# Routed tokens transposed one step ahead, and one spread of B and C for both halves of a state

## The chip, the cores and the metric

The kernel runs on one core of a Trainium2 chip. The metric is the device time of one launch in microseconds (us), the median of several runs. PE is TensorE (PEld its weight loads), DVE is VectorE, ACT is ScalarE, POOL is GpSimd, SP is SyncE. A line number L264 is a line of the kernel's file, as the profile gives it.

## What is computed

Two blocks on a residual stream x of 4 x 512 tokens, width 512. Each block adds a state-space layer over a context and then a feed-forward layer over the normalized x. The part in question is the second of these pieces together with the third: the mixture of experts of block 0, and the scan of block 1.

```
x = x + ssm0(ctx, layernorm(x))
x = x + moe(layernorm(x))       # shared expert + top 4 of 16 experts
x = x + ssm1(ctx, layernorm(x))
x = x + bitlinear_ffn(layernorm(x))

# ssm: per batch b, 512 channels, 16 states n, 512 time steps
u      = silu(conv(in_proj @ ctx))
delta  = softplus(dt_proj @ dt_lo + bias);  B, C = rows of x_proj @ u
state[e,n] = state[e,n] * exp(delta[e] * A[e,n]) + delta[e] * u[e] * B[n]
y[e]   = sum_n state[e,n] * C[n]  + D[e] * u[e]

# moe: token t, expert e of its top 4
out += coef[t,e] * (silu(x @ w1_e.T) * (x @ w3_e.T)) @ w2_e.T
```

B[n] and C[n] depend on the time step and not on the channel, so on the chip a row of 512 values is spread over 128 partitions before it is multiplied with a tile of channels.

## The kernel before

The kernel is a sequence of stages on one core, each with its own instruction order written out by hand for every engine; semaphores tie the engines together, and each engine takes its own queue strictly in order. The stages are the first scan (`ssm_first`, which also splits the expert weights into fp16 pairs and gets its C rows by DMA), a gate, the routing, `experts_and_ssm`, the combination of the routed outputs, a gate and the last feed-forward layer. The change lies in `experts_and_ssm` and in those parts of the class `Ssm` that the second scan uses; the branches with `alone` true belong to the first scan and keep their behaviour.

`experts_and_ssm` runs two things side by side. The feed-forward work is cut in slots: 88 slots of the shared expert (`NU`: 8 tiles of 256 tokens by 11 column pieces) and then 80 slots of routed steps g = 0 to 79 (`NSTEP`), each 128 gathered tokens of one expert. The scan work is cut in 148 entries, 37 for each of four batches, laid over the slots by `entry(slot)`: entries `at` 0 to 4 prepare a batch (in-projection, convolution, x_proj, dt, softplus), and 32 entries are the steps, one for each pair of a state n and a half of the channels (2 x 128 of 512). 68 entries lie in the shared slots, 58 of them steps; in the routed phase every slot has one, 70 of them steps, and two preparations begin at g = 6 and g = 43.

What a routed slot g does, by engine:

- PE: four fp32 transposes of the gathered tokens xg into the PSUM tile px (`x_transpose`, L1219); B of this scan step spread into pB by a matmul with a selector (`pe_spread_b`, L258); the down projection of step g-2 (L1227); three transposes of the hidden tile of g-1 (L1235, "hidden transposes" below); in a preparation the in-projection (`pe_in`); the up projection of g in 24 matmuls (L1246), in the middle of which C is spread into the same PSUM tile pB (`pe_spread_c`, L264); in a preparation then `pe_x` (L236) or `pe_dt` (L250).
- ACT: the high fp16 part of the tokens out of px (`x_hi`, L1333); the exponentials of the scan step (`act_exp`, L348); the copy of the down projection's result (L1349); the high part of the hidden tile (`h_hi`); the copy of C to SBUF (`act_c`, L341); tanh of the up result (L1343); then the preparation's work, such as `act_u` (L309), `act_z`, `act_e`, `act_ln`.
- DVE: the low part of the tokens (`x_lo`, L1446, reads px and xth); bu = du * B (`dve_bu`, L425); the scan (L434); the low part of the hidden tile (`h_lo`, L1451 and L1452); the two instructions of `silu_up` (L1457, L1460); then conv, split, delta and du (L413).
- POOL: the indirect fetch of the tokens of g+2 (L1149), the product of the scan's result with C (L471), the sum into U (L461).
- SP: the weights of the next expert into a ring of three, when an older expert is done.

The tiles xth and xtl exist once, px exists once, and the order of `x_transpose`, `x_hi`, `x_lo` and `up` is closed in one slot: `up(g)` waits for `x_lo(g)`. The shared slots have a similar chain with two buffers; four-transposes pieces there (`sx_transpose`, `sx_high`, `sx_low`) stand at the end of slots with column piece 4 or 7.

The scan step s is at first (batch, half, state): a batch goes through its 16 states for the first half of the channels and then for the second, so that B and C of a state are spread twice. B waits until the C before it is out of pB (`c_evac`), C waits until bu has read B (`bu_done`).

```
        def step(b, at):
            return b * STEPS + at - PRO, (at - PRO) // NS, (at - PRO) % NS
...
        pe.wait_ge(self.bu_done, s + 1)
        if not self.alone:
            pe.wait_ge(self.c_evac, s + 1)
```

## Time and profile before

| | |
|---|---|
| runs | 2286.73, 2280.6, 2284.96 us, median 2284.96 |
| profiled execution, its own time | 2281.42 us |
| its span in the trace | 2279.2 us |
| mean granted clock of PE | 0.876 |
| busy over the span | PE 1683.4 (74%), DVE 1759.7 (77%), ACT 1184.7 (52%), POOL 1336.8 (59%) |
| shared phase | about 797 to 1268 us |
| routed phase | about 1268 to 1896 us |

Busy shares over the span are means over stages with different limits; what a change in one stage is worth is read from that stage. In a timeline row a group of equal instructions in sequence is merged (x4), the us behind the start are the group's, and matmul times contain the drain, so the distance between starts is what a matmul holds PE for. PEclk in the table of stretches is the clock granted to PE as a share of 2.4 GHz.

### The profile page before, as it was taken

To read this page: it belongs to the slowest core of one execution; us is meant where nothing else is said; L and a number is where in the kernel's file an instruction comes from. 1 tells how busy PE (TensorE), PEld (TensorE's weight loads), DVE (VectorE), ACT (ScalarE), POOL (GpSimd) and SP (SyncE) were. 2 spreads that over 40 slices of the span, in tenths; PEclk is the share of its full clock that TensorE was granted. 3 is DMA by queue.
4 is the path that set the end of the run, shared out by engine and by line. 5 is a ranking of instruction groups with operands and counts; after the bars stand their busy time and mean duration, and the time that the engine had idled before them with its cause. 6 is when DMAs were issued, how large, how long until landed. Compare 5 with 4: busy or idle time off the path is not lost. (4 is left out here: it accounts for less than half of the span.)

```text
span 2279.2 us, 27596 instructions
## 1 busy us (share of the span) xinstructions
PE 1683.4 (74%) x8608; PEld 967.8 (42%) x8630; DVE 1759.7 (77%) x2275; ACT 1184.7 (52%) x1829; POOL 1336.8 (59%) x648
## 2 busy tenths in 40 slices
PE   4766756656536488999799988999889992005998
PEld 1222222212225445766467545666456661003554
DVE  4999999999955738887689847888478885757886
ACT  4675766757632034443444435555355551634776
POOL 0778778789950005775288815888258884653111
PEclk7878879889976588999899998999989996558999
DMA  6347456456544600001000333344424226650000
GB/s 213 132 149 236 149 169 222 152 177 223 182 143 134 144 24 10 11 13 35 5 10 30 135 113 137 121 157 159 144 95 157 81 75 249 210 170 1 24 24 28
DMA packets 127146, 264.65 MB, mean 116 GB/s; under 512 B 44546, under 2 KB 48386, under 8 KB 121794
## 3 DMA queue, kind: packets, MB, share of 16 engines
q1 hardware_dynamic: 93890, 184.24, 24.0%
q0 software_dynamic: 11520, 37.76, 5.8%
q10 hardware_dynamic: 21600, 40.90, 4.8%
q8 instruction: 78, 1.28, 0.2%
q14 instruction: 58, 0.48, 0.1%
HBM read 180.41 MB, written 82.44 MB: 115 GB/s over the span
## 5 line engine op out<-in xcount | busy, mean ns | idle before, releaser
L471 POOL TENSOR_TENSOR ssm_hs<-ssm_hs,ssm_Cs 128x1024 f32<-128x1024 f32 x128 | 314.9, 2461 | 144.7 <-DVE ssm_hs L434 140.7
L471 POOL TENSOR_TENSOR moe_hs<-moe_hs,moe_Cs 128x1024 f32<-128x1024 f32 x128 | 302.2, 2361 | 127.2 <-DVE moe_hs L434 96.1
L434 DVE TENSOR_TENSOR_SCAN moe_hs<-moe_dA,moe_bu 128x1024 f32<-128x1024 f32 x128 | 292.6, 2286 | 17.9 <-ACT moe_dA L348 8.4
L434 DVE TENSOR_TENSOR_SCAN ssm_hs<-ssm_dA,ssm_bu 128x1024 f32<-128x1024 f32 x128 | 292.8, 2287 | 17.4 <-ACT ssm_dA L348 0.5
L461 POOL TENSOR_TENSOR moe_U<-moe_U,moe_hs 128x1024 f32<-128x1024 f32 x128 | 302.0, 2360 | 5.9
L280 PE MATMUL ssm_pY<-ssm_hs,ssm_ident 128*128 128x512 f32 x512 | 276.9, 668 | 2.8 <-POOL ssm_hs L471 2.8
L1246 PE MATMUL moe_pgu<-all_Wreg,moe_xth 128*128 x1280 | 249.6, 318 | 31.4 <-DVE moe_xtl L1446 31.3
L1196 PE MATMUL moe_pgu<-moe_xsh,all_Wreg 128*128 128x256 f16 x1408 | 251.8, 277 | 10.9 <-DVE moe_hsl L1434 9.4
L258 PE MATMUL ssm_pB<-ssm_bc,ssm_sel 96*128 96x512 bf16 x128 | 54.9, 429 | 204.4 <-DVE ssm_bu L425 204.3
L1196 PE MATMUL moe_pgu<-moe_xsl,all_Wreg 128*128 128x256 f16 x704 | 195.0, 277 | 0.0
L666 POOL TENSOR_TENSOR ssm_wlo<-ssm_wst,ssm_whi 128x1360 f16<-128x1360 f32 x64 | 186.5, 2915 | 0.0
L348 ACT ACTIVATE ssm_dA<-ssm_dlt,ssm_A 128x511 f32<-128x511 f32 x256 | 169.0, 709 | 24.2 <-DVE ssm_hs L434 24.1
L348 ACT ACTIVATE moe_dA<-moe_dlt,moe_A 128x511 f32<-128x511 f32 x256 | 169.9, 714 | 18.3 <-DVE moe_du L413 18.3
L1246 PEld LDWEIGHTS moe_pgu<-all_Wreg,moe_xth 128*128 128x128 f16 x1280 | 127.0, 99 | 103.2 <-issue 36.9
L602 ACT ACTIVATE ssm_whi<-ssm_wst 128x1360 f16<-128x1360 f32 x64 | 85.5, 1336 | 155.4 <-DMA ssm_wst<-in_w_all 155.4
L425 DVE TENSOR_TENSOR ssm_bu<-ssm_du,ssm_pB 128x1024 f32<-128x1024 f32 x128 | 157.1, 1227 | 10.9 <-PE ssm_pB L258 0.8
L453 POOL TENSOR_TENSOR moe_U<-moe_U,moe_Dv 128x2048 f32<-128x2048 f32 x4 | 14.4, 3602 | 256.6 <-DVE moe_du L413 256.6
L425 DVE TENSOR_TENSOR moe_bu<-moe_du,moe_pB 128x1024 f32<-128x1024 f32 x128 | 156.3, 1221 | 6.8 <-PE moe_pB L258 6.7
L1196 PEld LDWEIGHTS moe_pgu<-moe_xsh,all_Wreg 128*128 128x128 f16 x1408 | 140.0, 99 | 40.6 <-issue 13.8
L280 PEld LDWEIGHTS ssm_pY<-ssm_hs,ssm_ident 128*128 128x128 f32 x512 | 111.2, 218 | 94.2 <-issue 85.2
L1246 PE MATMUL moe_pgu<-all_Wreg,moe_xtl 128*128 x640 | 150.3, 317 | 0.0
L1149 POOL DMA_INDIRECT moe_xg<-xn_d,all_idx x80 | 78.7, 983 | 120.7 <-PE moe_px L1219 110.3
(238 smaller groups left out, 3622.5 us busy)
## 6 DMA issues: line engine op xcount, KB each, us to landing
ssm_wst<-in_w_all SPq DMA_DIRECT2D x64, 680.0 KB, 4.9
w_hi<-ssm_whi SPq DMA_DIRECT2D x64, 340.0 KB, 2.3
w_lo<-ssm_wlo SPq DMA_DIRECT2D x64, 340.0 KB, 3.1
y_d<-moe_yo ACTq DMA_DIRECT2D x80, 256.0 KB
all_Wreg<-w_hi SPq DMA_DIRECT2D x16, 1088.0 KB
all_Wreg<-w_lo SPq DMA_DIRECT2D x16, 1088.0 KB
ssm_Cs<-c_d SPq DMA_DIRECT2D x64, 256.0 KB, 5.5
gate_Y<-y_ssm ACTq DMA_DIRECT2D x8, 1024.0 KB, 9.4
```

The source lines that it names most:

```text
L258: self.nc.tensor.matmul(self.pB[:], self.sel[:, ds(n, 1), :], self.bc3[:, b % self.dbl, :], start=True, stop=True).then_inc(self.b_rdy, 1)
L280: mm = self.nc.tensor.matmul(self.pY[k][:], self.ident[:], self.hs[:, j, k, :], start=False, stop=last, skip_group_check=True)
L348: ex = nc.scalar.activation(self.dA[:, q, k, 1:L], self.dlt[:, b % self.dbl, c, 1:L], ACT.Exp, scale=self.A[:, c, ds(n, 1)])
L425: self.nc.vector.tensor_tensor(self.bu[:], self.du[:, b % self.dbl, half * HC:(half + 1) * HC, :], self.pB[:].unsqueeze(1).to_broadcast([P ...
L434: self.nc.vector.tensor_tensor_scan(self.hs[:, j, :, :].rearrange("p k t -> p (k t)"), self.dA[:, q, :, :].rearrange("p k t -> p (k t)"), ...
L461: self.nc.gpsimd.tensor_tensor(Y, Y, self.hs[:, j, :, :], ALU.add).then_inc(self.acc_done, 1)
L471: self.nc.gpsimd.tensor_tensor(self.hs[:, j, :, :], self.hs[:, j, :, :], self.Cs[:, i:i + 1, :].to_broadcast([P, HC, L]), ALU.mult)\
L602: nc.scalar.activation(whi[:, k, :], wst[:, k, :], ACT.Copy, scale=WS).then_inc(hi_rdy, 1)
L666: nc.gpsimd.tensor_tensor(wlo[:, j % 2, :], wst[:, j % 2, :], whi[:, j % 2, :], ALU.subtract).then_inc(lo_rdy, 1)
L1149: nc.gpsimd.indirect_dma_start(out=xg[:, g % 2, :], out_offset=None, in_=r["xn_d"], in_offset=bass.IndirectOffsetOnAxis(ap=r["idx"][:, g:g ...
L1196: mm = nc.tensor.matmul(pgu[u % 2][:, q * TS:(q + 1) * TS], Ws[:, shared_place(c), z, o:o + P], xs[:, t % 2, k, :], start=(k == 0 and z == ...
L1246: mm = nc.tensor.matmul(ps, xt[:, k, :], w_of(w, z, P, k * 2 * IE + o, IE), start=(k == 0 and z == 0 and xt is xth), stop=(k == HK - 1 and ...
```

## The change

Four things are changed, all for the second scan and the routed steps.

- The step order becomes (batch, state, half): two steps in a row share a state. B is spread in front of the first of the two alone and stays in pB for both; C is spread once a state, in the slot of the second half for the next state (for the first state in the slot before the first step), and `act_c_pair` copies it into one of two buffers in place of four.
- The waits follow: B waits for the C copy of its own state, `dve_bu` for the B of its state, POOL for the C of its state, the C copy for the products of the state before the last.
- xth and xtl become double buffers (g % 2).
- `x_transpose`, `x_hi` and `x_lo` of g+1 move into slot g: on PE behind the hidden transposes of g-1 and ahead of `pe_in` and `up(g)`, on ACT behind `h_hi(g-1)` and ahead of the C copy and tanh, on DVE behind `h_lo(g-1)` and ahead of `silu_up(g)`. The slot before the first routed one does those of g = 0. px stays single, and the fetch of g+2 waits as before for the transposes of g.

```diff
@@ -128,7 +128,7 @@
...
-        self.Cs = m.sb("Cs", [P, NS if alone else R, L])
+        self.Cs = m.sb("Cs", [P, NS if alone else 2, L])
         self.dA = m.sb("dA", [P, ring, HC, L])
@@ -254,13 +254,13 @@
...
         if not self.alone:
-            pe.wait_ge(self.c_evac, s + 1)
+            pe.wait_ge(self.c_evac, s // 2 + 1)
         self.nc.tensor.matmul(self.pB[:], self.sel[:, ds(n, 1), :], self.bc3[:, b % self.dbl, :],
...
-        pe.wait_ge(self.bu_done, s + 2)
+        pe.wait_ge(self.bu_done, s + 1)
         self.nc.tensor.matmul(self.pC[:], self.sel[:, ds(n + NS, 1), :], self.bc3[:, b % self.dbl, :],
@@ -288,8 +288,6 @@
...
         nc.scalar.activation(self.A[:], self.alog[:], ACT.Copy, scale=-1.0).then_inc(self.a_neg, 1)
-        if not self.alone:
-            act.sem_inc(self.c_evac, 1)
         act.wait_ge(self.a_neg, 1)
@@ -335,10 +333,11 @@
...
-    def act_c(self, act, s, j):
-        act.wait_ge(self.c_rdy, s + 1)
-        act.wait_ge(self.prod_done, s + 1)
-        self.nc.scalar.copy(self.Cs[:, j, :], self.pC[:]).then_inc(self.c_evac, 1)
+    def act_c_pair(self, act, q):
+        act.wait_ge(self.c_rdy, q + 1)
+        if q >= 2:
+            act.wait_ge(self.prod_done, R + 2 * (q - 1))
+        self.nc.scalar.copy(self.Cs[:, q % 2, :], self.pC[:]).then_inc(self.c_evac, 1)
@@ -420,7 +419,7 @@
...
-        dve.wait_ge(self.b_rdy, s + 1)
+        dve.wait_ge(self.b_rdy, s + 1 if self.alone else s // 2 + 1)
         dve.wait_ge(self.scan_done, s + self.ring)
@@ -466,8 +465,8 @@
...
         else:
-            i = j
-            pool.wait_ge(self.c_evac, s + 2)
+            i = s // 2 % 2
+            pool.wait_ge(self.c_evac, s // 2 + 1)
         self.nc.gpsimd.tensor_tensor(self.hs[:, j, :, :], self.hs[:, j, :, :],
@@ -1050,8 +1049,8 @@
...
         xg = m.sb("xg", [P, 2, H])
-        xth = m.sb("xth", [P, HK, P], F16)
-        xtl = m.sb("xtl", [P, HK, P], F16)
+        xth = m.sb("xth", [P, 2, HK, P], F16)
+        xtl = m.sb("xtl", [P, 2, HK, P], F16)
         hth = m.sb("hth", [P, 3, P], F16)
@@ -1116,7 +1115,7 @@
...
-            return b * STEPS + at - PRO, (at - PRO) // NS, (at - PRO) % NS
+            return b * STEPS + at - PRO, (at - PRO) % 2, (at - PRO) // 2
@@ -1166,7 +1165,7 @@
...
                     else:
-                        S.pool_add(pool, b, (at - PRO - 1) // NS, s - 1, (s - 1) % R)
+                        S.pool_add(pool, b, 1 - half, s - 1, (s - 1) % R)
                     S.pool_step(pool, s, s % R)
@@ -1243,7 +1242,7 @@
...
                             for ps, o in ((pg, 0), (pu, IE)):
-                                mm = nc.tensor.matmul(ps, xt[:, k, :], w_of(w, z, P, k * 2 * IE + o, IE),
+                                mm = nc.tensor.matmul(ps, xt[:, g % 2, k, :], w_of(w, z, P, k * 2 * IE + o, IE),
                                                       start=(k == 0 and z == 0 and xt is xth), stop=(k == HK - 1 and xt is xtl))
@@ -1257,19 +1256,22 @@
...
                     def spread_b():
-                        if s is not None:
+                        if half == 0:
                             if at == PRO:
...
                     def spread_c():
-                        if s is not None:
-                            S.pe_spread_c(pe, b, s, n)
+
+                        if at == PRO - 1:
+                            pe.wait_ge(S.bc_split, 5 * (b + 1))
+                            S.pe_spread_c(pe, b, b * STEPS, 0)
+                        elif half == 1 and n + 1 < NS:
+                            S.pe_spread_c(pe, b, s + 1, n + 1)
...
                         need = pe.value_load(r["tab"][0:1, 0, g:g + 1], min_val=1, max_val=E)
-                        x_transpose(g)
                         spread_b()
@@ -1280,6 +1282,8 @@
...
                         spread_b()
+                    if -1 <= g < NSTEP - 1:
+                        x_transpose(g + 1)
                     if at == 0 or at == 1:
@@ -1330,7 +1334,7 @@
...
                     act.wait_ge(tx_rdy, g + 1)
-                    nc.scalar.activation(xth[:], px[:], ACT.Copy, scale=XS).then_inc(xh_rdy, 1)
+                    nc.scalar.activation(xth[:, g % 2, :, :], px[:], ACT.Copy, scale=XS).then_inc(xh_rdy, 1)
@@ -1361,8 +1365,6 @@
...
                         sh_high(slot - 1)
-                    if g >= 0:
-                        x_hi(g)
                     if s is not None:
@@ -1371,6 +1373,8 @@
...
                         h_hi(g - 1)
+                    if -1 <= g < NSTEP - 1:
+                        x_hi(g + 1)
                     if g >= 2:
@@ -1378,8 +1382,10 @@
...
                             sx_high(2 * (t + 1) + XT.index(c))
-                    if s is not None:
-                        S.act_c(act, s, s % R)
+                    if at == PRO - 1:
+                        S.act_c_pair(act, b * NS)
+                    elif half == 1 and n + 1 < NS:
+                        S.act_c_pair(act, s // 2 + 1)
                     if g >= 0:
@@ -1443,7 +1449,7 @@
...
                     dve.wait_ge(xh_rdy, g + 1)
-                    nc.vector.scalar_tensor_tensor(out=xtl[:], in0=px[:], scalar=XS, in1=xth[:],
+                    nc.vector.scalar_tensor_tensor(out=xtl[:, g % 2, :, :], in0=px[:], scalar=XS, in1=xth[:, g % 2, :, :],
                                                    op0=ALU.mult, op1=ALU.subtract).then_inc(xl_rdy, 1)
@@ -1469,8 +1475,6 @@
...
                     s, half, n = step(b, at) if at is not None and at >= PRO else (None, None, None)
-                    if g >= 0:
-                        x_lo(g)
                     if s is not None:
@@ -1493,6 +1497,8 @@
...
                         h_lo(g - 1)
+                    if -1 <= g < NSTEP - 1:
+                        x_lo(g + 1)
                     if g >= 0:
```

## Rows read from the trace of the kernel before

**Rows 1.** Busy time by stretch: us, each engine's busy (instructions), PEclk, DMA share, GB/s.
```profile
876.72:1058.33 181.61, 174.67 (x1287) 125.38 (x1286) 159.42 (x196) 85.82 (x180) 145.00 (x63) 1.00 0.03 10
...
1392.82:1601.46 208.64, 208.64 (x1304) 131.52 (x1303) 172.80 (x217) 119.57 (x249) 177.01 (x94) 1.00 0.42 146
...
1314.47:1392.82 78.35, 60.53 (x276) 32.19 (x275) 39.48 (x59) 32.88 (x55) 14.30 (x10) 0.87 0.31 110
1601.46:1681.36 79.90, 61.94 (x276) 32.74 (x275) 39.49 (x59) 32.88 (x56) 15.09 (x10) 0.85 0.29 102
```

**Rows 2.** Timeline, PE, one step: start, us, engine line operation out<-in [idle <-releaser].
```profile
1507.04 0.60 PE L1219 MATMUL moe_px<-moe_ident,moe_xg 128*128 128x128 f32 x4
...
1507.47 0.38 PE L258 MATMUL moe_pB<-moe_bc,moe_sel 96*128 96x512 bf16 x1
...
1509.64 0.49 PE L1235 MATMUL moe_pys<-moe_ident,moe_sgs 128*128 128x128 f32 x3
...
1509.97 0.76 PE L1246 MATMUL moe_pgu<-all_Wreg,moe_xth 128*128 x4
...
1511.76 0.38 PE L264 MATMUL moe_pB<-moe_bc,moe_sel 96*128 96x512 bf16 x1
...
1511.98 0.76 PE L1246 MATMUL moe_pgu<-all_Wreg,moe_xth 128*128 x4
...
1513.77 0.60 PE L1219 MATMUL moe_px<-moe_ident,moe_xg 128*128 128x128 f32 x4
```

**Rows 3.** Timeline, DVE and ACT in the same step.
```profile
1508.73 0.68 DVE L1446 SCALAR_TENSOR_TENSOR moe_xtl<-moe_px,moe_xth 128x512 f16<-128x512 f32 x1
...
1509.33 1.22 DVE L425 TENSOR_TENSOR moe_bu<-moe_du,moe_pB 128x1024 f32<-128x1024 f32 x1
...
1510.68 2.29 DVE L434 TENSOR_TENSOR_SCAN moe_hs<-moe_dA,moe_bu 128x1024 f32<-128x1024 f32 x1
...
1513.20 0.28 DVE L1452 TENSOR_TENSOR moe_htl<-moe_pys,moe_hth 96x128 f16<-96x128 f32 x1
...
1513.97 0.46 ACT L1343 ACTIVATE moe_sgs<-moe_pgu 128x352 f32<-128x352 f32 x1 [1.21 <-PE moe_pgu L1246]
...
1514.46 0.52 DVE L1457 SCALAR_TENSOR_TENSOR moe_sgs<-moe_sgs,moe_pgu 128x352 f32<-128x352 f32 x1 [0.99 <-ACT moe_sgs L1343]
...
1515.02 0.52 DVE L1460 SCALAR_TENSOR_TENSOR moe_sgs<-moe_pgu,moe_sgs 128x352 f32<-128x352 f32 x1
```

**Rows 4.** Waits from 1300 to 1870 us: waiter, releaser, us, times, longest.
```profile
PE moe_pgu L1246 <- DVE moe_xtl L1446: 31.3, 8, 6.9
```

**Rows 5.** Timeline, PE, the first scan preparation in the routed phase.
```profile
1345.26 1.35 PE L1246 MATMUL moe_pgu<-all_Wreg,moe_xth 128*128 x4 [6.65 <-DVE moe_xtl L1446]
...
1350.81 3.60 PE L236 MATMUL moe_bu<-moe_U,moe_w_x 128*112 128x512 f32 x8
...
1362.28 1.98 PE L250 MATMUL moe_bu<-moe_low,moe_w_up 16*128 16x512 f32 x4
...
1387.47 1.35 PE L1246 MATMUL moe_pgu<-all_Wreg,moe_xth 128*128 x4 [6.91 <-DVE moe_xtl L1446]
```

**Rows 6.** Timeline, ACT and DVE, same stretch, two rows.
```profile
1342.00 1.91 ACT L309 ACTIVATE moe_U<-moe_hs 128x2048 f32<-128x2048 f32 x1 [2.96 <-DVE moe_hs L376]
...
1385.50 1.23 DVE L413 TENSOR_TENSOR moe_du<-moe_dlt,moe_U 128x1024 f32<-128x1024 f32 x1
```

**Rows 7.** The indirect fetches of L1149: issue to landing.
```profile
DMA to landing us min/median/max: 3.2/3.6/5.8
```

**Rows 8.** Timeline, shared phase: two PE waits and two DVE scans.
```profile
910.85 0.38 PE L258 MATMUL moe_pB<-moe_bc,moe_sel 96*128 96x512 bf16 x1 [1.25 <-ACT moe_Cs L341]
...
984.64 2.29 DVE L434 TENSOR_TENSOR_SCAN moe_hs<-moe_dA,moe_bu 128x1024 f32<-128x1024 f32 x1 [0.27 <-ACT moe_dA L348]
...
989.43 2.29 DVE L434 TENSOR_TENSOR_SCAN moe_hs<-moe_dA,moe_bu 128x1024 f32<-128x1024 f32 x1 [0.27 <-ACT moe_dA L348]
...
1123.23 0.61 PE L264 MATMUL moe_pB<-moe_bc,moe_sel 96*128 96x512 bf16 x1 [4.93 <-DVE moe_bu L425]
```

## The prediction

> **What bounds the kernel now.** The table by stretch comes first, because the second scan shares its stage with two kinds of feed-forward work. In the routed phase 31 ordinary steps fill 208.64 us, 6.73 us each, and PE is busy for all 208.64 of it at a granted clock of 1.00 (2.4 GHz); DVE has 172.80 (5.57 a step) and POOL 177.01 (5.71) [rows 1]. So PE sets the pace there and whatever leaves PE's queue is gained in full, until DVE or POOL is reached. The timeline of one step shows the same without a hole: transposes at 1507.04, the B spread at 1507.47, the two down groups, the hidden transposes at 1509.64, up from 1509.97 to 1513.77 with the C spread inside [rows 2]. A spread holds PE for 0.22 us (1511.76 to 1511.98).
>
> The two stretches in which a batch's scan is prepared (at 0 to 4, and the first step) are different: six slots take 78.35 and 79.90 us, where six ordinary ones take 40.4, and PE is busy for only 60.53 and 61.94 of it [rows 1]. The list of waits says for what: up waited 31.3 us in 8 times for x_lo [rows 4]. The two long ones are 6.65 and 6.91 us, and the matmuls behind them run at half clock for a while [rows 5]: the up that started at 1345.26 ended at 1350.81, 5.55 us against 3.58 (1509.97 to 1513.77, less the spread). The reason is order in the queue: x_hi of slot g stands on ACT behind the preparation work of slot g-1 (act_u until 1343.91 [rows 6]), x_lo on DVE behind conv, delta and du (until 1386.73).
>
> The shared phase (88 slots, 58 of them with a step) is mixed: over 181.61 us PE is busy for 174.67 and DVE for 159.42, to which some 0.27 us waits for ACT in a row of steps belong [rows 1, 8]. Within such a row DVE takes 4.79 us a step (984.64 to 989.43), PE about 4.35; the slot without a step lets DVE catch up.
>
> **The change, part by part.**
>
> *Spreads.* 32 B and 32 C a batch become 16 and 16: 128 matmuls of 0.22 us, 28.2 us of PE in all, and 64 copies of C on ACT, which has idle time and counts nothing. Of the 70 steps in the routed phase, four are counted with the preparations below; 66 x 0.22 = **14.5 us**. I take it whole. The check is DVE. Counted from the end of up (1507.04), silu_up now ends at about 1.77 (1515.54 less 1513.77) [rows 3]. New order: bu 1.72 to 2.94, scan 3.05 to 5.35 (as now 1.35 behind bu), h_lo to 5.9, the moved x_lo to 6.55, tanh of the next up at 6.51 + 0.20 to 7.17. PE needs 6.51 a step and DVE is through 0.6 earlier. Even a scan that stays where it is (it ends at 1512.97, h_lo at 1513.48) has x_lo done at 7.05. Hidden transposes need silu_up at 1.77; PE comes to them at 1.95 in a second-half step, only 0.2 later. POOL has 5.71 of 6.51.
>
> *x ahead.* 80 times the four transposes, x_hi and x_lo are the same instructions, one slot earlier, so in ordinary steps nothing is gained but the spread. In a preparation I follow the chain. (1) The up of 1345.26 needs no x_lo from its own slot and runs right behind the hidden transposes; pe_x then waits for act_u and starts at about 1344.0 where it now starts at 1350.81 [rows 5, 6]: 6.8 gained. (2) From pe_x to pe_dt are now 11.47 us; the work in it is 3.4 + 2.7 + 3.6 = 9.7 (pe_x; down, hidden and x transposes; up), the rest is one of the smaller x_lo waits. pe_dt comes 8.6 earlier. (3) act_z and act_e follow as now, but x_hi and x_lo no longer stand ahead of dve_t; du ends about 10 us earlier, at 1376.7 instead of 1386.73. (4) PE has then run ahead: four dt matmuls (5.5 us with their waits), two slots of about 6.5 and short waits end at about 1373.5, and there it waits for something new: the down of two slots ago needs h_lo, which stands on DVE behind bu and scan and on ACT behind exp. That is du's end + exp 1.3 or bu 1.2 + scan 2.3 + h_lo 0.7, about 4.5 us. Then a slot of 6.5 us, and 2 us more because after some 7 us of waiting PE again runs at half clock, as in [rows 5]: 13.0 us from du to the end of the second step's up. Now it is 12.6 (1386.73 over 1387.47, 5.15 at half clock, then 6.73). So 10 - 0.4 = **9.7 us** for the first. The second takes 79.90 now, 1.5 more by a longer time at half clock; I give it 11. Together **21 us** (bounds: 2 x 3 if step 3 gives everything back, 2 x 13 if the clock stays up).
>
> *Fetches.* The transposes of g+1 now stand in slot g, so a fetch of L1149 has less time: POOL issues it at about 1.7 of a slot, it is needed at 8.8, 7.1 us later, where it had 11. It lands in 3.2 to 5.8 [rows 7]. Cost 0, with 1.3 us to spare over the worst row. The Trainium skill ("DMA: Bandwidth & Descriptors", "Issuing engines are not separate DMA queues") speaks against such a move: what POOL issues interleaves with SP's weight loads on the same engines. The worst row was measured with those loads running, so the sum goes by the row; by the rule taken hard it would be the slower rival below.
>
> *Shared phase.* 54 ordinary steps x 0.22 = 11.9. A C copy that stands behind sx_high holds up the next B by 1.25 us [rows 8]; of six such places two fall on first-half steps, which have no C now: 2.5. At each batch's first step PE waited 4.93 us for bu before C [rows 8]; that C now comes a slot earlier, but the next one waits for the second bu, so I count 1.5 each, 3. Against this DVE: its 159.42 + 4.7 us of a stretch that would shrink to about 172 leave little room, and with 4.79 against 4.13 a fourth step in a row must wait, as must down groups for sh_y. I take 3 off: **14 us** (bounds 3 and 18).
>
> **Sum.** 14.5 + 21 + 14 = 49.5, say 50. The profiled execution took 2281.42 us, so 2231.5; the median of the runs shown is 3.5 above it: **2235 us**. Everything behind this stage only moves.
>
> **Rivals.**
>
> *The preparation gives its gain back* (the new wait for h_lo, a clock that falls more often). For it: PE cannot pass that wait, and the two half-clock rows. Against: the chain through act_u and pe_dt gets shorter by itself. 6 instead of 21: 2250.
>
> *The shared phase stays bound by DVE*, 3 instead of 14: 2246. For it the 4.79, against it that DVE idles in every slot without a step.
>
> *More than I count*: no half clock and all 18 of the shared phase, 2225.
>
> *Nothing changes*: PE's matmuls would have to be off the path; a PE busy for 208.64 of 208.64 excludes it nearly. 2285.
>
> *Slower: fetches land late.* Only if landing takes over 7.1 us; were each of 16 weight loads to hold up one fetch so that it takes twice the worst row, 11.6, PE would wait 4.5 x 16 = 72 us: 2235 + 72 = 2307. It decides against the change once the wait is over 50 / 16 = 3.1 us, a landing of 10.2. No fetch came near.
>
> The Trainium skill ("TensorE: Matmul & The Clock Gate", "Why this matters for your kernels") warns of idle gaps between bursts of matmuls, after which the clock is halved. The trace agrees (5.55 against 3.58 behind 6.65 us of idling); the first rival's price stands without it.
>
> **Chances and range.** The forecast 0.60, own range 2224 to 2246; gain given back 0.16; DVE-bound shared phase 0.08; more 0.10; nothing 0.02; slower 0.04. Up to 2256 both smaller-gain rivals are in, down to 2220 the larger: low 2220, high 2256. About 0.3% is what a measurement of this kernel can tell from no change. Faster 0.94, same 0.02, slower 0.04.
>
> **What would show it.** 64 rows each for L258 and L264. Ordinary routed steps alternate around a mean of 6.51, PE still busy throughout; 6.6 or more with PE waiting for silu_up or htl would put DVE in the place of PE. No wait of up for x_lo; instead one of down (L1227) of some 7 us per preparation; six slots in 66 to 69 us. A wait of the x transposes for xg would be the slower rival; its landing row tells. In the shared phase waits for bu grow behind C in second-half steps, and the 4.93 us before C is gone. The prediction is wrong if the routed steps stay at 6.73 or the wait for htl is over 15 us.

## The result and the profile after

The changed kernel takes 2233.05 us, median of 4 runs (2232.16 to 2235.33), beside 2284.05 us for the kernel before: a ratio of 0.9776, 95% interval 0.9764 to 0.9788, so 51 us faster. The forecast was 2235 us, the range 2220 to 2256.

The profiled execution took 2233.23 us, its span is 2231.4. Most lines of the file stand one to six numbers from where they stood before: down is L1226, the hidden transposes L1234, up L1245, tanh L1347, h_lo L1457 and L1458, x_lo L1452, silu_up L1463 and L1466, the fetch L1148, bu L424, the scan L433.

The table by stretch answers to [rows 1]; columns as there. The first row is the shared phase between the same two slots as before (8 to 48), then the first preparation, 30 ordinary steps, the second preparation, 30 ordinary steps; a preparation is given with seven slots here, from tanh to tanh, and not with the six of [rows 1]: six took 66.0 and 65.7 us (forecast 66 to 69), but the seventh took 10.08 and 11.15 where an ordinary slot takes 6.51, so six alone would flatter the change.

```profile
877.65:1053.75 176.10, 168.46 (x1259) 122.57 (x1258) 158.71 (x195) 77.41 (x164) 144.67 (x63) 1.00 0.04 10
1300.88:1376.98 76.10, 65.04 (x316) 35.44 (x315) 44.88 (x66) 36.45 (x64) 22.06 (x14) 0.91 0.34 121
1376.98:1572.08 195.10, 195.10 (x1230) 123.11 (x1229) 167.28 (x210) 104.16 (x224) 169.30 (x90) 1.00 0.44 153
1572.08:1648.93 76.85, 65.88 (x316) 35.72 (x315) 45.08 (x66) 36.56 (x64) 23.52 (x15) 0.89 0.31 113
1648.93:1843.59 194.66, 194.66 (x1226) 122.57 (x1224) 166.69 (x209) 103.66 (x224) 165.82 (x87) 1.00 0.34 114
```

An ordinary step takes 6.50 us (195.10 / 30) and PE is still busy for all of it; DVE has 5.58, POOL 5.64. The same seven slots of the preparations took 85.09 and 86.63 us before. These are windows of the same view of the kernel before, the first one from 1314.47 and the second from 1601.46:

```profile
1314.47:1399.56 85.09, 67.27 (x318) 36.44 (x317) 45.06 (x66) 36.75 (x64) 19.90 (x13) 0.88 0.31 108
1601.46:1688.09 86.63, 68.67 (x318) 36.98 (x317) 45.06 (x66) 36.74 (x63) 19.73 (x13) 0.86 0.28 100
```

The timeline of PE in an ordinary step after (the step of a second half, with the C spread in its up; the B spread in the last row opens the step of the next first half) answers to [rows 2]. The step takes 6.51 us (1487.46 to 1493.97); one spread stands in each step.

```profile
1487.46 0.59 PE L1226 MATMUL moe_pys<-all_Wreg,moe_hth 128*128 x2
...
1489.40 0.49 PE L1234 MATMUL moe_pys<-moe_ident,moe_sgs 128*128 128x128 f32 x3
1489.73 0.60 PE L1218 MATMUL moe_px<-moe_ident,moe_xg 128*128 128x128 f32 x4
1490.17 0.76 PE L1245 MATMUL moe_pgu<-all_Wreg,moe_xth 128*128 x4
...
1491.96 0.38 PE L264 MATMUL moe_pB<-moe_bc,moe_sel 96*128 96x512 bf16 x1
...
1493.97 0.38 PE L258 MATMUL moe_pB<-moe_bc,moe_sel 96*128 96x512 bf16 x1
```

DVE in the same step, to be held against [rows 3]: silu_up ends 1.77 us behind the end of up (1487.46), bu runs from 1.69 to 2.91, the scan from 3.04 to 5.33, x_lo ends at 6.44.

```profile
1488.71 0.52 DVE L1466 SCALAR_TENSOR_TENSOR moe_sgs<-moe_pgu,moe_sgs 128x352 f32<-128x352 f32 x1
1489.15 1.22 DVE L424 TENSOR_TENSOR moe_bu<-moe_du,moe_pB 128x1024 f32<-128x1024 f32 x1
1490.50 2.29 DVE L433 TENSOR_TENSOR_SCAN moe_hs<-moe_dA,moe_bu 128x1024 f32<-128x1024 f32 x1
...
1493.22 0.68 DVE L1452 SCALAR_TENSOR_TENSOR moe_xtl<-moe_px,moe_xth 128x512 f16<-128x512 f32 x1
```

The list of waits from 1290 to 1820 us has no row of up for x_lo, where [rows 4] had 31.3 us in 8 times. A wait that was not there is now the longest of PE:

```profile
PE moe_pys L1226 <- DVE moe_htl L1458: 14.0, 2, 7.0
```

The first preparation on PE, against [rows 5]: x_proj (L236) starts 29.49 us behind the start of the stretch where it started 36.34 behind it (1350.81 less 1314.47), the dt matmuls (L250) at 39.40 where they stood at 47.81, and the new wait is 7.00 us long.

```profile
1330.37 3.69 PE L236 MATMUL moe_bu<-moe_U,moe_w_x 128*112 128x512 f32 x8 [1.76 <-ACT moe_U L307]
...
1340.28 1.98 PE L250 MATMUL moe_bu<-moe_low,moe_w_up 16*128 16x512 f32 x4
...
1368.65 1.03 PE L1226 MATMUL moe_pys<-all_Wreg,moe_hth 128*128 x2 [7.00 <-DVE moe_htl L1458]
1369.48 0.63 PE L1226 MATMUL moe_pys<-all_Wreg,moe_htl 128*128 x1
...
1376.78 0.38 PE L258 MATMUL moe_pB<-moe_bc,moe_sel 96*128 96x512 bf16 x1
```

DVE in the same place shows what down waited for: the last du, bu, the scan, and only then h_lo.

```profile
1363.03 1.22 DVE L412 TENSOR_TENSOR moe_du<-moe_dlt,moe_U 128x1024 f32<-128x1024 f32 x1
1364.29 1.23 DVE L424 TENSOR_TENSOR moe_bu<-moe_du,moe_pB 128x1024 f32<-128x1024 f32 x1
1365.71 2.29 DVE L433 TENSOR_TENSOR_SCAN moe_hs<-moe_dA,moe_bu 128x1024 f32<-128x1024 f32 x1 [0.19 <-ACT moe_dA L347]
...
1368.23 0.28 DVE L1458 TENSOR_TENSOR moe_htl<-moe_pys,moe_hth 96x128 f16<-96x128 f32 x1
```

**A ruler for the experiments.** ACT's tanh rows mark all 168 slots. The distances between them, in us, by stretch ("steady" are slots 8 to 48 and 56 to 87 of the shared phase; "starts" 0 to 8 and 48 to 56, where a batch is prepared and takes its first step; "passage" is slot 87 to 88, "ordinary" twice 30 routed steps, "prep." the seven slots of each preparation):

| kernel | median us | starts | steady | passage | prep. | ordinary |
|---|---|---|---|---|---|---|
| before | 2284.05 | 69.38, 71.50 | 181.61, 138.08 | 13.31 | 85.09, 86.63 | 201.90, 201.90 |
| changed | 2233.05 | 65.18, 68.37 | 176.10, 136.08 | 10.41 | 76.10, 76.85 | 195.10, 194.66 |
| changed, again | 2234.96 | 67.68, 70.24 | 176.13, 136.43 | 10.40 | 76.82, 75.86 | 195.10, 194.67 |
| spreads only | 2252.40 | 65.18, 68.37 | 176.12, 135.61 | 11.48 | 85.61, 85.15 | 195.08, 195.08 |
| tokens ahead only | 2256.10 | 67.11, 70.67 | 181.60, 138.55 | 10.62 | 75.05, 74.75 | 201.90, 201.47 |
| B every step | 2246.28 | 67.65, 69.32 | 177.13, 137.53 | 12.08 | 76.84, 75.94 | 198.38, 197.94 |
| before, short silu | 2272.19 | 69.16, 71.20 | 178.63, 136.52 | 10.66 | 85.51, 85.17 | 201.90, 201.90 |
| changed, short silu | 2227.24 | 65.60, 69.44 | 171.78, 132.92 | 10.16 | 75.72, 76.68 | 195.10, 194.66 |
| C copy first | 2230.38 | 65.18, 67.18 | 173.92, 133.88 | 10.41 | 76.98, 75.94 | 195.10, 194.67 |
| hidden tile first | 2227.62 | 65.53, 69.05 | 176.20, 136.40 | 10.40 | 75.61, 74.61 | 195.10, 194.67 |
| feed-forward first | 2233.28 | 67.66, 70.25 | 176.13, 136.42 | 10.40 | 73.25, 72.14 | 197.58, 199.97 |
| both of these | 2236.33 | 66.29, 70.43 | 174.07, 134.25 | 12.09 | 72.44, 72.66 | 199.71, 199.98 |
| fetch behind the sum | 2274.90 | 66.43, 68.82 | 176.20, 136.41 | 12.08 | 80.79, 81.17 | 215.99, 205.53 |
| best, fetch early | 2223.81 | 66.31, 70.46 | 174.05, 134.25 | 12.09 | 72.44, 71.19 | 195.89, 195.45 |

Steady and ordinary stretches repeat to some 0.4 us from one execution to the next. The starts don't: 65.18 and 67.68 are the same kernel. The passage takes 10.4 or 12.1 us in kernels that are alike there. So a difference of 2 us in the starts or the passage shows nothing. (Both of these = feed-forward first and C copy first.)

### The profile page after: what moved, and what is told of

It is laid out like the page before. It is cut to its first block and busy times, and to the rows that moved or that the text cites. A ratio compares the mean times of both kernels' runs of the same rounds, so it can differ in the third digit from the quotient of the medians.

```text
span 2231.4 us, 27149 instructions
## 1 busy us (share of the span) xinstructions
PE 1653.2 (74%) x8480; PEld 954.2 (43%) x8502; DVE 1758.9 (79%) x2275; ACT 1143.2 (51%) x1765; POOL 1337.3 (60%) x648
## 5 line engine op out<-in xcount | busy, mean ns | idle before, releaser
L433 DVE TENSOR_TENSOR_SCAN moe_hs<-moe_dA,moe_bu 128x1024 f32<-128x1024 f32 x128 | 292.6, 2286 | 20.0 <-ACT moe_dA L347 10.1
L433 DVE TENSOR_TENSOR_SCAN ssm_hs<-ssm_dA,ssm_bu 128x1024 f32<-128x1024 f32 x128 | 292.7, 2287 | 17.3 <-ACT ssm_dA L347 0.5
L1195 PE MATMUL moe_pgu<-moe_xsh,all_Wreg 128*128 128x256 f16 x1408 | 255.3, 279 | 12.8 <-DVE moe_hsl L1440 11.3
L1245 PE MATMUL moe_pgu<-all_Wreg,moe_xth 128*128 x1280 | 243.6, 313 | 0.0
L424 DVE TENSOR_TENSOR ssm_bu<-ssm_du,ssm_pB 128x1024 f32<-128x1024 f32 x128 | 157.1, 1227 | 10.6 <-PE ssm_pB L258 0.5
L1226 PE MATMUL moe_pys<-all_Wreg,moe_hth 128*128 (+1 forms) x480 | 148.3, 391 | 15.4 <-DVE moe_htl L1458 15.4
L424 DVE TENSOR_TENSOR moe_bu<-moe_du,moe_pB 128x1024 f32<-128x1024 f32 x128 | 156.2, 1220 | 3.1 <-PE moe_pB L258 2.8
L1245 PEld LDWEIGHTS moe_pgu<-all_Wreg,moe_xth 128*128 128x128 f16 x1280 | 125.4, 98 | 63.4 <-issue 2.3
L1245 PE MATMUL moe_pgu<-all_Wreg,moe_xtl 128*128 x640 | 147.7, 313 | 0.0
```

The lines of the kernel that those rows point to most:

```text
L424: self.nc.vector.tensor_tensor(self.bu[:], self.du[:, b % self.dbl, half * HC:(half + 1) * HC, :], self.pB[:].unsqueeze(1).to_broadcast([P ...
L433: self.nc.vector.tensor_tensor_scan(self.hs[:, j, :, :].rearrange("p k t -> p (k t)"), self.dA[:, q, :, :].rearrange("p k t -> p (k t)"), ...
L1195: mm = nc.tensor.matmul(pgu[u % 2][:, q * TS:(q + 1) * TS], Ws[:, shared_place(c), z, o:o + P], xs[:, t % 2, k, :], start=(k == 0 and z == ...
L1226: mm = nc.tensor.matmul(py[:], ht[0:n, q, :], w_of(w, z, n, HK * 2 * IE + q * H, H), start=(q == 0 and z == 0 and ht is hth), stop=(q == 2 ...
L1245: mm = nc.tensor.matmul(ps, xt[:, g % 2, k, :], w_of(w, z, P, k * 2 * IE + o, IE), start=(k == 0 and z == 0 and xt is xth), stop=(k == HK ...
```

## The experiments

My theory was the prediction's sum: spreads in the ordinary steps and the shared phase, tokens ahead in the preparations, each by itself and additive. Its rivals were that the two hide each other, that DVE bounds the shared phase, and that the fetches have no room left.

**Spreads only.** The changed kernel with the tokens' work back in its own slot, xth and xtl single.

```diff
+                        x_transpose(g)
                         spread_b()
...
-                    if -1 <= g < NSTEP - 1:
-                        x_transpose(g + 1)
```

> The changed kernel with the x transposes, x_hi and x_lo put back into their own slot and single xth and xtl: the spreads alone. Theory (the parts add up: 0.22 us of PE for each spread left out, and the preparations shorten only through x ahead): ordinary routed slots at 6.51 us, up waits again some 31 us for x_lo in 8 waits, the six preparation slots at 78 to 80 us, the shared phase as in the changed kernel; about 2284 - 15 - 14.8 = 2254 us. Rival (the freed C spread of the first step also shortens the preparations): 2245 or less, with the preparation slots under 75 us. Rival (the ordinary slots gained by x ahead and not by the spreads): slots of 6.7 us, 2268.

2252.4 us, ratio to before 0.9868 (0.9852 to 0.9884): 31.7 us of the 51. The ordinary steps and the steady shared slots are those of the changed kernel to 0.5 us, the preparations those of before, and up waits for x_lo as before:

```profile
PE moe_pgu L1245 <- DVE moe_xtl L1451: 33.1, 8, 6.9
```

**Tokens ahead only.** The kernel before with the three moves and double xth and xtl. With C in four buffers the tiles don't fit: two more fp16 token tiles need 2 KB a partition, and only the 4 KB that the change frees by two C buffers give that room. So C has three buffers here, and its copy waits for one product more. The two parts of the change are not independent in this sense: the spreads pay for the memory of the token tiles.

```diff
-        self.Cs = m.sb("Cs", [P, NS if alone else R, L])
+        self.Cs = m.sb("Cs", [P, NS if alone else 3, L])
...
+                    if -1 <= g < NSTEP - 1:
+                        x_transpose(g + 1)
```

> The kernel before with x ahead and double xth and xtl, step order and spreads untouched; C has three buffers instead of four, to make room. Theory: ordinary routed slots stay at 6.73 us; up no longer waits for x_lo, down waits some 7 us once in each preparation; the two preparations give 19 to 20 us and the passage from the shared to the routed phase 3; about 2284 - 22 = 2262 us. Rival (without the earlier C the preparations gain less): over 2268. Rival (the two parts need each other and more than add up): e1 and this one together leave more than 5 us of the measured 51 unexplained.

2256.1 us, ratio 0.9885 (0.9869 to 0.9902): 28.1 us. Ordinary steps are those of before; the preparations are 10.0 and 11.9 shorter. They are also 1.1 and 2.1 shorter than those of the changed kernel, though they hold more spreads. PE's timeline says why: its wait comes inside up, at the C spread, for bu, and not at down for h_lo.

```profile
1376.84 0.61 PE L264 MATMUL moe_pB<-moe_bc,moe_sel 96*128 96x512 bf16 x1 [5.72 <-DVE moe_bu L425]
1377.24 1.38 PE L1246 MATMUL moe_pgu<-all_Wreg,moe_xth 128*128 x4
```

The last du ends at 1375.53 there and the up of the second step at 1387.13, 11.6 later; in the changed kernel it is 1364.25 to 1376.78, 12.5. Waiting in the middle of up, PE comes back 1.3 us behind du and not 4.4 (behind bu, not behind scan and h_lo), has only half an up left, and finds h_lo done when it reaches down. The medians' gains of both parts alone sum to 59.8, 8.8 more than both together; by the ratios, each good to about 4 us, it is 56.4, 5.3 more. The slots account for 4.1 of it in the preparations (some 1 of them the scatter of the spreads-only kernel there), 1.6 in the passage and 3.1 in the starts; passage and starts of one kernel differ by as much from one execution to the next. So what is shown of the loss is about 3 us in the preparations.

**B spread for every step**, C once a state.

```diff
-        dve.wait_ge(self.b_rdy, s + 1 if self.alone else s // 2 + 1)
+        dve.wait_ge(self.b_rdy, s + 1)
...
-                        if half == 0:
+                        if half is not None:
```

> The changed kernel, but B spread again for the second half: 64 matmuls of 0.22 us more on PE, C once a state. Theory (routed slots are bound by PE, shared slots mostly by DVE): routed second-half slots 6.73, first-half 6.51, 7.7 us more there, and 1 to 3 us more in the shared phase; 2233 + 10 = 2243. Rival (the shared phase is bound by PE too): 6.4 us more there, 2247. Rival (PE is not the bound of the routed slots): 2235 or less.

2246.28 us, ratio 0.9837 (0.9821 to 0.9853). The ordinary stretches are 3.28 longer, 15 spreads of 0.22, as each term of the routed sum says. The rest of the 11 to 13 us over the changed kernel is in the shared phase: 1.0 and 1.5 in the steady parts, and 1.7 in the passage, 2.5 and 1.0 in the starts, where such a difference shows nothing. The steady parts hold 28 of the added spreads, 6.2 us of PE, and grew by 2.5: over half of what a spread costs there disappears in PE's waits (those for bu fall from 4.1 to 1.6 us). That answers the rival on record: the steady shared slots are bound by PE only in part.

**The changed kernel again**, measured beside C copy first, feed-forward first and both together.

> The changed kernel once more, as the measure for the three beside it on the same chip: 2233 us, ratio 0.977 to 0.979. Its profile also shows whether the lengths of the slots and of the waits are the same from one execution to the next.

2234.96 us, ratio 0.9786 (0.9772 to 0.9799).

**Does DVE count in the shared phase?** Both kernels with one DVE instruction of the shared slots cut: in `sh_silu_up` the product of gate and sigmoid is done for 16 of 256 columns, the others are left out. It takes 153 ns where it takes 403, so each shared slot has 0.25 us less of DVE. The routed slots are untouched.

```diff
-  nc.vector.scalar_tensor_tensor(out=s_, in0=s_, scalar=1.0, in1=g_,
+  nc.vector.scalar_tensor_tensor(out=s_[:, 0:16], in0=s_[:, 0:16], scalar=1.0, in1=g_[:, 0:16],
```

> The kernel before with the first of the two silu instructions of the shared expert cut to 16 of 256 token columns (the product with 1 + tanh is left out for the others): about 0.3 us less on DVE in each of 88 shared slots, nothing less on PE. Theory (before the change PE bounds the shared phase): 0 to 2 us less. Rival (DVE bound it already then): 5 us or more less. The same cut on the changed kernel is to be compared with this one.

> The changed kernel with the first of the two silu instructions of the shared expert cut to 16 of 256 token columns (the product with 1 + tanh is left out for the others): about 0.3 us less on DVE in each of 88 shared slots, nothing less on PE. Theory (after the change DVE bounds a good part of the shared phase: its waits for bu and sh_y grew by some 5 us): 3 to 6 us less than the changed kernel, and clearly more than the same cut gives on the kernel before. Rival (the rest of the shared phase's missing gain is ACT's or the half clock): 0 to 2 us, as on the kernel before.

Before: 2272.19 (0.995, 0.9933 to 0.9968), steady shared slots 4.5 shorter. After: 2227.24 (0.9749, 0.9731 to 0.9767), steady shared slots 7.5 shorter (4.3 and 3.2). I had expected 0 to 2 for before: that was wrong. DVE's queue held back some shared slots already before the change, and more of them after it. This rests on the steady slots and their waits; the medians don't show it, they fell by 12 before and by 6 to 8 after. Of the 12, 4.5 are in the steady slots and 2.7 in the passage; the rest is spread over stretches that differ between executions.

**The C copy ahead of the token conversion** in shared slots.

```diff
-                        t, c = divmod(slot, CSH)
-                        if c in XT and t + 1 < NTS:
-                            sx_high(2 * (t + 1) + XT.index(c))
                     if at == PRO - 1:
                         S.act_c_pair(act, b * NS)
                     elif half == 1 and n + 1 < NS:
                         S.act_c_pair(act, s // 2 + 1)
+                    if g < 0:
+                        t, c = divmod(slot, CSH)
+                        if c in XT and t + 1 < NTS:
+                            sx_high(2 * (t + 1) + XT.index(c))
```

> In the shared slots ACT copies C before sx_high. Theory: the four waits of 1.25 us of B for the C copy behind sx_high go away. If PE bounds the slots around them: 4 to 5 us less than the changed kernel. If DVE bounds them: 1 to 2 us less, and waits for bu grow instead.

2230.38 us beside 2234.96, ratios 0.9768 (0.9754 to 0.9783) and 0.9786 (0.9772 to 0.9799): the intervals overlap, but the slots are plain, 2.2 and 2.5 shorter, as where PE bounds them. The four waits of 1.25 us behind sx_high are gone; the two of 1.90 us that stay lie in the starts. The wait that it was made for, between 860 and 1250 us, in the changed kernel and then in this one:

```profile
PE moe_pB L258 <- ACT moe_Cs L340: 8.8, 6, 1.9
```
```profile
PE moe_pB L258 <- ACT moe_Cs L340: 3.8, 2, 1.9
```

**Who should stand first at a batch's first step?** First h_hi and h_lo alone ahead of exp, bu and scan, then all feed-forward work of the slot (h, x, tanh, silu) ahead of them.

```diff
+                    early = g >= 1 and at == PRO
+                    if early:
+                        h_lo(g - 1)
                     if s is not None:
```
```diff
                     if g >= 0:
                         silu_up(g)
+                    if late:
+                        dve.wait_ge(S.d_step, S.d_count(b + 1, 0))
+                        S.dve_bu(dve, b, half, s)
+                        S.dve_scan(dve, s, s % R)
```

> Only y_evac, h_hi and h_lo stand ahead of exp, bu and scan in the slot of a batch's first step. Theory: down starts about 3.7 us earlier, but the hidden transposes then wait for silu_up, which stays behind the scan: a wait of about 3 us there, 2 us less in each preparation, 4 us less than the changed kernel. Rival (no wait behind the next one): 7 us less.

> In the slot of a batch's first step, ACT does y_evac, h_hi, x_hi and tanh before exp, and DVE h_lo, x_lo and silu_up before bu and scan. Theory (PE idles 7 us in down because h_lo stands behind bu and scan on DVE, and up runs at half clock after it): the wait of down falls to about 3 us, a new wait of 2 us at C for bu appears, 2.5 to 4 us less in each of the two preparations, 5 to 8 us less than the changed kernel, 2226. Rival (the chain through DVE is full, and its work only changes order): within 1.5 us of the changed kernel.

The first takes 2227.62 us (0.9748, 0.973 to 0.9766), its preparations 0.5 to 2.2 shorter; the hidden transposes waited 1.0 us for silu_up in the first preparation, not the 3 forecast; the median is lower by more than the slots explain. The second takes 2233.28 (0.9763, 0.975 to 0.9777) and not 2226, the time of the changed kernel as its rival said, but not for the rival's reason: the wait of down fell to 3.3 us and its preparations are 3 to 5 us shorter than those of the changed kernel. Single slots behind them took 8.99 and 11.82 us in place of 6.51. PE's row names the cause; then the fetch on POOL and the weight load on SP that belong to it, and the landing row of the fetches of that stretch:

```profile
1398.73 0.44 PE L1218 MATMUL moe_px<-moe_ident,moe_xg 128*128 128x128 f32 x2 [2.27 <-DMA moe_xg<-xn_d,all_idx]
...
1390.32 0.98 POOL L1148 DMA_INDIRECT moe_xg<-xn_d,all_idx  x1 [0.16 <-issue]
...
1389.88 0.32 SPq L1138 DMA_DIRECT2D all_Wreg<-w_hi  x1
```
```profile
DMA to landing us min/median/max: 3.3/3.4/8.4
```

With the scan put last, POOL comes out of the preparation late and works without a gap for six steps; so this fetch is issued 0.44 us behind the weight load and lands after 8.4 us. It also comes late itself: PE was ready for it 6.1 us after its issue, where an ordinary slot of the changed kernel leaves 7.2 to 7.6. In the changed kernel the same pair stands the other way round, the fetch 0.96 us ahead of the load, and it landed after 3.6:

```profile
1391.20 0.98 POOL L1148 DMA_INDIRECT moe_xg<-xn_d,all_idx  x1
...
1392.16 0.32 SPq L1138 DMA_DIRECT2D all_Wreg<-w_hi  x1
```

**Both orders at once** (C copy first and feed-forward first):

> The two changes of order together. If they are independent: the sum of the two gains, 2221 to 2230 us.

2236.33 us, 0.9791 (0.9777 to 0.9804), outside the 2221 to 2230 forecast. Steady slots and preparations came out as short as in the two kernels alone, and the late fetches took it back: two waits of 1.96 and 2.81 us, slots of 10.36 and 11.04. Each wait is followed by half clock; behind the shorter one:

```profile
1398.68:1402.64 3.96, 3.96 (x16) 2.24 (x17) 2.05 (x4) 0.60 (x1) 3.80 (x3) 0.57 0.34 126
```

**The fetch behind POOL's sum**, 2.4 us later in the changed kernel.

```diff
-                    if 0 <= g < NSTEP - 2:
-                        pool.wait_ge(tx_rdy, g + 1)
-                        fetch(g + 2)
+                    def next_fetch():
+                        if 0 <= g < NSTEP - 2:
+                            pool.wait_ge(tx_rdy, g + 1)
+                            fetch(g + 2)
...
                         S.pool_add(pool, b, 1 - half, s - 1, (s - 1) % R)
+                        next_fetch()
                     S.pool_step(pool, s, s % R)
```

> The changed kernel with the indirect fetch of the tokens of g+2 behind the sum on POOL instead of ahead of it, 2.4 us later in each slot; tests the slower rival. Theory (it is needed 7.1 us after its present issue and lands 3.6 to 5.8 us after it): 4.7 us are left, so only the fetches that run beside a weight load come late, some 15 waits of the x transposes of up to 1.1 us; 0 to 10 us more than the changed kernel. Rival (the margin is larger than reckoned): no wait and no difference. Rival (the margin was nearly used up): over 30 us more.

2274.9 us, 0.9955 (0.9937 to 0.9973): 42 us lost, four fifths of the gain. The waits from 1240 us on:

```profile
PE moe_px L1222 <- DMA moe_xg<-xn_d,all_idx: 26.8, 11, 3.5
```

Of the 14 weight loads from 1266 us on, 13 have their fetch 0.47 to 1.72 us behind them and one 1.07 ahead. The 11 waits follow 11 of the 13; the two without a wait lie in a preparation, where a slot is long. The trace has no landing times for these fetches; from the issue to the end of the wait pass 7.4 to 8.6 us, and but for the first, PE was ready after 4.9 to 5.3. The window of 3 us behind one such load (1401.31), with the DMA share and GB/s at the end, shows what the fetch shares the engines with:

```profile
1403.00:1406.00 3.00, 3.00 (x21) 1.88 (x20) 2.39 (x4) 0.34 (x1) 2.41 (x2) 1.00 0.94 382
```

The waits sum to 26.8 us, and the eleven slots are together 42.0 us longer than those of the changed kernel. Nearly all of the rest is PE's clock. Two of the waits, 2.35 and 2.74 us long, and the stretch right behind each (PEclk is the third number from the end):

```profile
1410.25 0.66 PE L1222 MATMUL moe_px<-moe_ident,moe_xg 128*128 128x128 f32 x4 [2.35 <-DMA moe_xg<-xn_d,all_idx]
...
1480.62 0.65 PE L1222 MATMUL moe_px<-moe_ident,moe_xg 128*128 128x128 f32 x4 [2.74 <-DMA moe_xg<-xn_d,all_idx]
```
```profile
1410.25:1412.50 2.25, 2.25 (x16) 1.66 (x17) 1.75 (x4) 0.60 (x1) 1.66 (x2) 1.00 0.44 139
1480.62:1484.50 3.88, 3.88 (x17) 2.19 (x17) 1.36 (x4) 0.60 (x1) 3.56 (x2) 0.58 0.44 136
```

The slot with the first took 9.08 us, 0.2 more than step and wait together, the slot with the second 11.13, 1.9 more.

**The best version**: both orders, and the fetch one place earlier than in the changed kernel.

```diff
-                    if 0 <= g < NSTEP - 2:
-                        pool.wait_ge(tx_rdy, g + 1)
-                        fetch(g + 2)
+                    def next_fetch():
+                        if -1 <= g < NSTEP - 3:
+                            pool.wait_ge(tx_rdy, g + 2)
+                            fetch(g + 3)
...
                         S.pool_add(pool, b, 1 - half, s - 1, (s - 1) % R)
+                        next_fetch()
```

> The changed kernel with three edits: at the first step of a batch the feed-forward work of the slot (hidden tile, tokens, tanh and silu) stands ahead of exp, bu and scan; in shared slots the copy of C stands ahead of the token conversion; and the fetch of step g+3 stands behind POOL's sum of slot g, ahead of its product, where the fetch of g+2 opened the slot. Without the third edit the same kernel took 2236.33 us: its ordinary slots of 6.51 us had four of 7.29 to 11.04, at the places where PE waited for a fetch. Theory: those stalls are a fetch that POOL issues 0.4 to 1.7 us behind the issue of a weight load, which then lands after 7.4 to 8.4 us instead of 3.3 to 3.6, against 7.1 to 7.4 between issue and need. With the fetch one place earlier there are some 10 us between issue and need (4.8 us into a slot, needed 2.3 us into the slot after next: 13.0 + 2.3 - 4.8 = 10.5), so no wait of the transposes is left, each slot behind the two preparations is 6.51 again, and the time is 2236.3 less 0.8 + 3.9 + 0.8 + 4.5 = 10 and some half clock behind them: 2222 to 2227. Rival one: the landing grows with the earlier issue, since every fetch now comes 2 to 3 us behind the issue of a weight load where most came before it; then some 16 slots wait again and the time stays at 2236 or more. Rival two: POOL, which must now wait for the transposes of g+1 between its sum and its product, delays the scan's buffers: ordinary slots over 6.51 and waits of the scan, 2240 or more.

2223.81 us (5 runs, 2217.49 to 2225.77), 0.9735 (0.9718 to 0.9752): 60 us under before, 9 under the changed kernel, and 12.5 under the same orders with the fetch where it was. No wait for a fetch is left, though nearly every fetch beside a weight load now comes 1.0 to 3.4 us behind it; one of them, with its load, and the transposes that read it two slots on (1550.24, 11.45 us later):

```profile
1538.79 0.99 POOL L1148 DMA_INDIRECT moe_xg<-xn_d,all_idx  x1
...
1537.08 0.32 SPq L1138 DMA_DIRECT2D all_Wreg<-w_hi  x1
...
1550.24 0.60 PE L1222 MATMUL moe_px<-moe_ident,moe_xg 128*128 128x128 f32 x4
```

The longest landing that the trace has between 1400 and 1600 us is 7.8. The slot of 7.30 us behind each preparation stayed, against what I had written. PE's rows show where it lies:

```profile
1371.92 0.38 PE L258 MATMUL moe_pB<-moe_bc,moe_sel 96*128 96x512 bf16 x1 [0.36 <-issue]
1372.39 0.60 PE L1230 MATMUL moe_pys<-all_Wreg,moe_hth 128*128 x2
```

The B spread starts 0.5 us late, with a gap for which the profile names no releaser, and down starts 0.47 behind it where 0.22 is usual, just behind the end of h_lo (1372.25). The clock is at 1.00. What holds the spread stays open.

## Why the prediction was right

*Ordinary steps* (14.5 forecast). 6.73 became 6.51 in each of them: 6.8 and 7.2 in the two stretches of 30 and 1.0 in the five ahead of the first preparation, 15.0. DVE's new times are those of the prediction to 0.1 us.

*Preparations* (9.7 and 11). 9.0 and 9.8, by the seven slots. Step 1: x_proj 6.85 earlier (6.8). Step 2: dt 8.4 earlier (8.6). Step 3: the end of du 8.9 earlier (10): this is the term that was too large. ACT's last preparation work stands behind a tanh at 1355.17, and down and hidden transposes of that slot ran at half clock behind the dt matmuls (1345.58 to 1350.03, 4.5 us where 2.3 are usual), which the sum didn't have. Step 4: wait of down 7.0 us (some 7), from du to the end of the second step's up 12.5 (13.0). The rival "gives its gain back" is out: 19 of 21 are there. But with tokens ahead alone the wait falls in a better place, and the two parts together lose 3 us of that.

*Shared phase* (14). 14.8 in the profiled execution and 10.1 in the second one of the same kernel, by other terms than mine. The steady slots repeat, 7.5 and 7.1 shorter, where 11.9 + 2.5 - 3 = 11.4 was reckoned. The spreads are there (56 fewer, 12.3 us), and so are the 2.5: the waits for the C copy fell from six, 7.5 us, to four, 5.0. The term that was too small is the 3 for DVE. The waits in slots 8 to 48 before, then after:

```profile
PE moe_pB L258 <- ACT moe_Cs L341: 5.0, 4, 1.3
PE moe_pys L1208 <- DVE all_X L1441: 1.4, 2, 0.7
PE moe_pB L264 <- DVE moe_bu L425: 0.2, 1, 0.2
```
```profile
PE moe_pB L264 <- DVE moe_bu L424: 3.0, 5, 0.8
PE moe_pB L258 <- ACT moe_Cs L340: 2.5, 2, 1.3
PE moe_pys L1207 <- DVE all_X L1447: 2.2, 2, 1.4
```

Over both steady stretches the waits for DVE (bu, and sh_y in the row of all_X) grew from 2.4 to 7.7 us, 5.3 where I took off 3. 12.3 + 2.5 - 5.3 = 9.5; the last 2 us are in gaps too short for a row. The kernels with the short silu point to DVE for them too: there these rows fall by 5.5 and 2.4 us and the slots by 7.5 and 4.5. In the starts 7.3 came in place of 3, but only 3.0 in the second execution. The 4.9 us wait for bu ahead of C is gone, but B now waits 1.90 us for the C copy once in each start, and up waits longer for the low part of the shared hidden tile (9.4 us became 11.3 and 14.0). With the copy of C first, 4.4 to 4.8 us came back in the steady slots.

*DVE.* The rival "bound by DVE" (3 in place of 14) is wrong in size and right in kind: cutting 0.25 us a slot gains 7.5 in the steady slots after and 4.5 before.

*Passage.* The first routed slot lost its own transposes and x_lo; 13.31 became 10.41. I had not counted it. Part of it is clock: before, 2.96 us of waiting for the hidden tile are followed by half clock, and the kernel before with the short silu has 10.66 there, behind a wait of 1.92 us. So how much of the 2.9 is the change's is not shown.

*Sum.* Stage 51.5 (1082.7 to 1031.1 between first and last tanh) against 49.5. The profiled execution of after entered the stage 5.1 us later (812.5 against 807.3) and was 1.4 us shorter behind it, so its span is 47.8 less. The second execution of the changed kernel gives 47.1 for the stage. The 2235 against 2233.05 is closer than its terms: the starts gave 4 us more than forecast in one execution and nothing more in the other, the passage up to 2.9 that were not in the sum, and the steady slots 4 less. That these nearly cancel is luck; the ordinary steps and the preparations, 34 of the 51.5 us of the stage, are not.

*The fetches* (cost 0). Right in the number, by luck in part. I took 5.8, the worst landing of before, as measured with the weight loads running. It was not: the fetches of 5.80 and 5.60 us were issued in a preparation 0.67 us behind the scan's own write of 1024 KB (y_ssm), 14 us behind the last weight load. In the ordinary slots of before the fetch stood on the lucky side of each weight load, 1.0 us or more ahead of it, and landed after at most 3.9. In the changed kernel's ordinary slots ten of the weight loads are issued 0.7 to 1.0 us *behind* a fetch, which then lands after 3.5 to 5.6 us; two of its loads, both in a preparation, stand 1.0 and 1.7 us ahead of the fetch, and these landed after 8.0 us, over the 7.1 I had set as the limit:

```profile
DMA to landing us min/median/max: 3.3/3.6/8.0
```

They cost nothing only because the next transposes that read them came 20 and 21 us after the issue. The other kernels show the price where the slots are short: put the fetch 0.4 to 1.9 us behind the load, and it lands after 7.4 to 8.4 us in the slots where PE waited, while a fetch that is late itself leaves 4.7 to 6.1. So the mechanism of the slower rival is real. Its price was too high (a landing of 7.4 to 8.4, not 11.6), and the landing of 10.2 from which it should decide was too lenient: 11 waits of 2.4 us on average cost 42 us, 3.8 each, since half clock came behind the longer ones. The rule of the Trainium skill that I weighed ("DMA: Bandwidth & Descriptors", "Issuing engines are not separate DMA queues": what POOL issues runs on the same engines as SP's loads and interleaves with them) agrees with these rows. Here the order of issue decides how much.

## What to carry to other kernels

A transfer's landing time read from the trace of before belongs to the order of issue of before. Ahead of moving its consumer or its issue, look at which side of the large loads it stands on; if it can slide behind one, take the landing behind a load as its time, or fetch one step further ahead, as the best version does.

A prefetch takes a conversion out of the queue only to let the engine run to the next wait. Name that wait: here it was the one for h_lo, and what stood ahead of h_lo on DVE (bu and scan, 3.7 us from 1364.29 to the end of the scan) was worth 3 to 5 us a preparation once all feed-forward work of the slot stood ahead of it.

Part gains add up only as long as no part moves another's stall. Run each part alone, and look slot by slot, since medians can't tell where 9 us went.

## What the runs showed that I had not expected

How long the indirect fetch of 128 token rows takes depends on where it is issued beside the two weight loads of 1088 KB. All fetches from 1275 us on, in all kernels here, that have a landing time in the trace:

| issue of the fetch | landing, us | fetches |
|---|---|---|
| 0.95 to 1.01 us ahead of the first load | 3.4 to 4.1 | 66 |
| 0.73 to 0.80 ahead | 4.4 to 6.3 | 46 |
| 0.57 ahead | 6.6 to 6.7 | 4 |
| 0.4 to 1.9 behind | 7.0 to 8.8 | 26 |
| 5 to 6.5 behind | 3.7 to 6.2 | 112 |

Between the first two rows a quarter of a microsecond of lead is worth 1 to 2 us of landing. In the window shown above, within such a load, the DMA engines are 94% busy.

In the kernel with the fetch behind the sum, PE's waits of 2.08 to 2.35 us left its clock at 1.00; those of 2.61 to 3.45 us were followed by half clock (0.58 over 3.9 us behind the one of 2.74). The slots show it: 8.81 to 9.08 us with the shorter waits, 11.01 to 12.84 with the longer ones in ordinary slots. So the longer stalls cost 1.7 to 1.8 times themselves. But the length of the wait alone doesn't decide it: with both orders at once a wait of 1.96 us was followed by half clock (0.57 over 3.96 us). What does decide it stays open.

The same kernel differs by up to 2.5 us in the first eight slots of the stage between executions, while ordinary steps repeat to 0.01 us. The changed kernel's two executions had PE's clock at 0.92 and 0.90 over these slots, and up waited 1.6 us longer for the shared hidden tile in the slower one; I haven't found what starts it.
